# Expert attention: subtraction and row sums on VectorE, one exponential per eight heads, another order of pieces

## The chip, the core and the metric

The kernel runs on one NeuronCore of a Trainium2 chip. The metric is the device time of one execution in microseconds (us). Engines that matter here: TensorE (matmuls and transposes; PE in the rows, with PEld for its weight loads), VectorE (DVE), ScalarE (ACT), GpSimd (POOL) and SyncE (SP), which issues most transfers. Each engine works through its own queue in order, and engines wait for each other through semaphores.

## The reference, cut to what matters

Two decoder layers over 32 sequences of 112 tokens and 256 features. The last piece is a mixture of experts whose expert is a whole encoder layer; each sequence uses 2 of 4 experts, so there are 64 items (sequence, expert) to compute.

```python
def _encoder_layer(x, iw, ib, ow, ob, l1w, l1b, l2w, l2b, n1w, n1b, n2w, n2b):
    qkv = x @ iw.T + ib                        # 16 heads of 16
    scores = jnp.einsum('bhqd,bhkd->bhqk', q, k) / scale      # scale = 4
    attn = jax.nn.softmax(scores, axis=-1)
    o = jnp.einsum('bhqk,bhkd->bhqd', attn, v)...
    o = o @ ow.T + ob
    x = _layernorm(x + o, n1w, n1b)
    ff = jax.nn.relu(x @ l1w.T + l1b) @ l2w.T + l2b
    return _layernorm(x + ff, n2w, n2b)
gate_logits = x.mean(axis=1) @ gate_w.T + gate_b
_, top_idx = jax.lax.top_k(gate_logits, K)                    # K = 2
return jnp.einsum('be,ebsd->bsd', gate_weights * mask, expert_outs)
```

## The kernel before

The kernel has three stages, one after the other: the first layer, the first part of the second layer, and the experts. All is fp32. Only the third stage is touched.

In the third stage four lanes (`LANES`, 0 to 3) work through 16 items each (`share`). A lane has its own tiles, two PSUM banks (`bps0` to `bps3` in the profile) and its own copy of an expert's weights (`wexp`, `rexp`), which SyncE loads anew only where the next item of the lane has another expert. For one item of a lane:

- TensorE transposes the input (L1604), computes q and k feature-major (L1610) and v (L1626).
- VectorE adds the output bias to the input (L1819) and builds `QM`, q spread over masked heads (L1822, two instructions).
- For each of two groups of eight heads (`c`): TensorE computes the scores, 112x112 a head, into the lane's two banks (L1638). VectorE takes the maximum of each row (L1830, `mx`) and multiplies it by -0.25 (L1831, `low`). ScalarE computes exp(0.25 s + low), one instruction a head, with the row sum through its accumulator (L1716, `sums`); the profile shows an ACTIVATION_READ_ACCUMULATOR behind each. VectorE takes the reciprocal of the sums (L1834) and multiplies it in (L1835). TensorE transposes the probabilities (L1650), ScalarE copies them back (L1722).
- TensorE multiplies by v (L1658) and by the output weights (L1665). VectorE adds to the residual (L1840) and computes the layer norm: statistics (L1801, L1802), variance (L1803), normalisation (L1807, it waits for the inverse root that GpSimd computes, L1872), scale and shift (L1810, L1811), and the second bias (L1847).
- TensorE transposes (L1604) and runs the two layers of the feed-forward part (L1610 with ScalarE's relu L1739, and L1681). VectorE adds (L1850), does the second layer norm in the same way, multiplies by the gate (L1858), and GpSimd adds the item to the output by a transfer (L1885).

A half softmax below is what one lane does for one group of eight heads.

What an engine does for one item is written once, as a generator (`batch`) that yields between pieces. `run_slots` interleaves the four lanes' pieces on each engine: a piece of lane s is put at the turn (0 to 999) that the table `TURNS` gives for it, shifted by the lane's `lead3`. That makes the loop body; it runs 15 times. `FIRST` and `LAST` give the turns of what stands before the loop and behind it. So these tables alone set the order of the instructions on each queue. The rows named sp3, pe3, act3, dve3 and pool3 are the third stage's.

Semaphores that the change touches: `top_ready` (VectorE tells that the maxima are there), `exp_ready` (ScalarE tells that the exponentials are), `soft_ready`, and `s_psum` (the scores are in PSUM). The next scores may overwrite the banks, and the transposes may, once the exponentials have read them: TensorE waits for `exp_ready`.

Each VectorE instruction that needs the result of the one before it waits on a semaphore for it (`chained`).

Of the kernel before, what the change touches and what calls it, by code (L numbers as in the profile page):

```python
# [9 lines left out]
ALU = mybir.AluOpType  # L10
ACT = mybir.ActivationFunctionType
# [5 lines left out]
H = 16  # L17
# [23 lines left out]
def offsets(parts):  # L41
    at, out = 0, {}
    for name, w in parts:
# [122 lines left out]
            (),  # L166
            (),
            (820,)),
    "pe3": ((),
            (686, 763, 882, 982,),  # L170
            (526, 607, 687, 870, 944,),
            (236, 298, 399, 602, 745, 933, 973, 973,)),
    "act3": ((),
             (734, 885, 923,),
             (519, 587, 655, 887, 937,),
             (351, 427, 427, 598, 842, 930, 936, 964,)),
    "dve3": ((),
             (743, 886, 968,),
             (514, 666, 760, 816, 932,),
             (285, 497, 613, 613, 751, 914, 953,)),  # L180
    "pool3": ((),
              (),
              (960,),
              (878, 935, 961,)),
# [139 lines left out]
def build(nc, x, ctx, mask, wa, ca, ra, up, we, re_, gb, kc, kb, rtc, out, xmid, lg, mrow, sel, nb=B):  # L324
    with ExitStack() as es:
# [1110 lines left out]
        with ExitStack() as phase:  # L1436
# [40 lines left out]
            mx, low, sums, rec = lanes("mx", [T, H]), lanes("low", [T, H]), lanes("sums", [T, H]), lanes("rec", [T, H])  # L1477
# [107 lines left out]
            def _(pe):  # L1585
# [12 lines left out]
                def batch(s, at):  # L1598
# [30 lines left out]
                    for c in range(C2):  # L1629
                        yield  # L1630
                        if c == 0:
                            t.wait(masked_ready[s], 2)
                            t.wait(vx_read[s])
                        else:
                            t.wait(exp_ready[s])
# [5 lines left out]
                    for c in range(C2):  # L1641
                        yield
                        t.wait(soft_ready[s])
                        if c == 0:
                            t.wait(exp_ready[s])
                        else:
                            t.wait(pt_ready[s])
# [38 lines left out]
            def _(act):  # L1686
# [5 lines left out]
                def batch(s, at):  # L1692
# [17 lines left out]
                    for c in range(C2):  # L1710
                        yield
                        t.wait(top_ready[s])
                        for i in range(2):
                            for v in range(4):
                                h = 8 * c + 4 * i + v
                                m = A(PT[s][0:T, h, :], bank[s][i][0:T, v * T:(v + 1) * T], ACT.Exp, scale=0.25, bias=low[s][:, h:h + 1],  # L1716
                                      accum_out=sums[s][:, h:h + 1])
                        m.then_inc(exp_ready[s], 1)
# [25 lines left out]
            def _(dve):  # L1744
# [46 lines left out]
                def batch(s, at):  # L1791
# [34 lines left out]
                    for c in range(C2):  # L1826
# [4 lines left out]
                        v.tensor_scalar(low[s][:, eight], mx[s][:, eight], -0.25, None, ALU.mult).then_inc(top_ready[s], 1)  # L1831
                        yield
                        t.wait(exp_ready[s])
                        chained(v.reciprocal(rec[s][:, eight], sums[s][:, eight]))  # L1834
# [146 lines left out]
```

## Time and profile before

| | us |
|---|---|
| median of 3 runs | 3574.93 |
| lowest, highest | 3574.05, 3575.97 |
| profiled execution, its time | 3580.41 |
| profiled execution, its span | 3578.8 |
| busy in the span: matmuls | 3349.6 (94%) |
| VectorE | 2125.6 (59%) |
| ScalarE | 1943.2 (54%) |
| GpSimd | 375.7 (10%) |

The span runs from the first to the last instruction. The busy shares are averages over three stages with different loads. The third stage starts at about 2490 us and lasts to the end. A wait is put down to the instruction that released it. Matmuls are pipelined, and in the third stage each fp32 matmul of the code shows as two records.

### The profile page before, as it was taken

How to read it: one execution, taken by the hardware profiler on the slowest of the kernel's cores; microseconds unless marked ns; L12 is line 12 of the kernel's file. 1: busy time of each engine (PE TensorE's matmuls, PEld its weight loads, DVE VectorE, ACT ScalarE, POOL GpSimd, SP SyncE). 2: the span in 40 equal slices, each digit the busy share in tenths (PEclk: the TensorE clock that was granted, in tenths of full speed). 3: DMA queues.
4: the chain of work that ended last, by engine and by line, in shares of the span. 5: the costliest groups of instructions: out<-in, count | busy, mean ns of one | idle time of the engine just before them, and what ended most of it. 6: DMA issues, size and time to landing. Idle time of an engine off the chain costs nothing. (4 is left out here: it accounts for less than half of the span.)

```text
span 3578.8 us, 81208 instructions
## 1 busy us (share of the span) xinstructions
PE 3349.6 (94%) x30471; PEld 2507.5 (70%) x30471; DVE 2125.6 (59%) x6898; ACT 1943.2 (54%) x6528; POOL 375.7 (10%) x455
## 2 busy tenths in 40 slices
PE   6999999999799999999999999994999998999998
PEld 4777777777566666666666665663888887888887
DVE  4666666666444545454554545462777776777776
ACT  3655556555244444545454444542777775766775
POOL 1111111111000000000000000000011111111111
PEclk9999999999799999999999999997999999999999
DMA  2000000000200000000000000004100012120000
GB/s 82 13 13 17 13 13 13 14 15 8 98 7 22 18 18 22 18 22 18 22 18 20 19 15 25 15 2 144 56 14 15 13 35 60 29 58 14 14 13 13
DMA packets 63555, 94.47 MB, mean 26 GB/s; under 512 B 7763, under 2 KB 59603, under 8 KB 62147
## 3 DMA queue, kind: packets, MB, share of 16 engines
q1 hardware_dynamic: 55074, 83.41, 7.5%
q0 software_dynamic: 8224, 7.36, 1.8%
q8 instruction: 195, 3.19, 0.4%
q14 instruction: 62, 0.50, 0.0%
HBM read 72.07 MB, written 18.37 MB: 25 GB/s over the span
## 5 line engine op out<-in xcount | busy, mean ns | idle before, releaser
L1377 DVE CUSTOM_DVE_ANT_0 PON<-pps,PMR 112x375 f32<-112x375 f32 x512 | 259.7, 545 | 278.2 <-PE pps L1097 277.4
L1610 PE MATMUL bps<-BXT,Bwexp 128*128 128x112 f32 x3072 | 374.4, 279 | 15.1 <-DMA Bwexp<-in_we 7.5
L1610 PEld LDWEIGHTS bps<-BXT,Bwexp 128*128 128x128 f32 x3072 | 360.7, 194 | 36.9 <-ACT BXT L1732 15.9
L1716 ACT ACTIVATE BPT<-bps,Blow 112x112 f32<-112x112 f32 x1024 | 349.1, 392 | 15.2 <-DVE Blow L1831 14.7
L1230 ACT ACTIVATE PPT<-pps,mcol 125x896 f32<-125x896 f32 x192 | 193.3, 1007 | 196.9 <-PE pps L1116 196.4
L1716 ACT ACTIVATION_READ_ACCUMULATOR BPT<-bps,Blow 112x1 f32 x1024 | 250.1, 246 | 0.0
L1681 PE MATMUL bps<-Bwexp,BPT 128*112 128x256 f32 x1024 | 235.3, 381 | 0.0
L1097 PE MATMUL pps<-PKT,PQM 64*112 64x375 f32 x1024 | 226.4, 522 | 2.5 <-DVE Pmx L1377 1.5
L800 POOL TENSOR_TENSOR rstd<-var,nhalf 112x1 f32<-112x1 f32 (+1 forms) x96 | 149.5, 1557 | 745.3 <-DVE var L718 504.1
L1410 POOL TENSOR_TENSOR Prstd<-Pvar,nhalf 112x1 f32<-112x1 f32 x128 | 71.4, 560 | 1395.6 <-DVE Pvar L1297 1395.6
L643 ACT ACTIVATE PT<-PT,low 112x112 f32<-112x112 f32 x512 | 191.0, 384 | 36.3 <-DVE low L775 36.3
L1681 PEld LDWEIGHTS bps<-Bwexp,BPT 128*112 128x112 f32 x1024 | 176.2, 176 | 40.2
L1116 PE MATMUL pps<-PQM,PKT 64*125 64x448 f32 x768 | 187.4, 566 | 0.0
L1305 DVE TENSOR_TENSOR PX<-PX,pps 112x256 f32<-112x256 f32 x96 | 40.2, 419 | 229.0 <-PE pps L972 138.1
L1739 ACT ACTIVATE BPT<-bps,Bwexp 128x112 f32<-128x112 f32 x512 | 137.7, 386 | 35.0 <-PE bps L1610 35.0
L1872 POOL TENSOR_TENSOR Brstd<-Bvar,nhalf 112x1 f32<-112x1 f32 x128 | 74.2, 586 | 761.3 <-DVE Bvar L1803 761.3
L1722 ACT ACTIVATE BPT<-bps 112x896 f32<-112x896 f32 x128 | 120.5, 941 | 56.6 <-PE bps L1650 56.1
L1830 DVE TENSOR_REDUCE Bmx<-bps 112x8 f32<-112x896 f32 x128 | 139.0, 1086 | 19.2 <-PE bps L1638 18.0
L1835 DVE TENSOR_TENSOR BPT<-BPT,Brec 112x896 f32<-112x896 f32 x128 | 139.7, 1092 | 4.4
L474 PEld LDWEIGHTS ps<-CT,wa_sb 128*128 128x128 f32 x1024 | 131.7, 205 | 11.5 <-issue 1.6
L474 PEld LDWEIGHTS ps<-XT,wa_sb 128*128 128x128 f32 x1024 | 123.8, 198 | 21.4 <-issue 18.8
L1638 PE MATMUL bps<-BKT,BQM 64*112 64x112 f32 x2048 | 134.1, 270 | 4.0 <-ACT BPT L1716 2.4
(288 smaller groups left out, 7336.4 us busy)
## 6 DMA issues: line engine op xcount, KB each, us to landing
Bwexp<-in_we SPq DMA_DIRECT2D x7, 2304.0 KB, 15.7
PCX<-in_ctx SPq DMA_DIRECT2D x32, 375.0 KB
BXIN<-xmid SPq DMA_DIRECT2D x64, 112.0 KB
out<-BY POOLq DMA_DIRECT2D x64, 112.0 KB, 2.9
Bwexp<-in_we SPq DMA_DIRECT2D x7, 777.0 KB, 4.9
wa_sb<-in_wa SPq DMA_DIRECT2D x1, 4736.0 KB, 14.5
Brexp<-in_re SPq DMA_DIRECT2D x7, 672.0 KB
XIN<-in_x SPq DMA_DIRECT2D x32, 112.0 KB
```

What stands on the lines that cost most here:

```text
L474: m = mm(bk[:, j * T:(j + 1) * T], wt[:, c, m2 * 128:(m2 + 1) * 128], rhs[:, c, :], start=(c == 0), stop=(c == C2 - 1))
L643: m = A(PT[s][:, h, :], PT[s][:, h, :], ACT.Exp, bias=low[s][:, h:h + 1], accum_out=sums[s][:, h:h + 1])
L800: g.tensor_tensor(rstd[s][:, 0:n], var[s][:, 0:n], nhalf[0:T, 0:n], ALU.pow).then_inc(rstd_ready[s], 1)
L1097: m = mm(bank[s][i][0:T, 0:LC], QM[s][side[i], r // 4, r % 4, :], KT[s][side[i], r // 4, :], start=True, stop=True)
L1116: m = mm(bank[s][i][0:KP, 0:QW], KT[s][side[i], c, k * KP:(k + 1) * KP], QM[s][side[i], c, :, :], start=False, stop=True, skip_group_check ...
L1230: A(PT[s][0:KP, k, :, :].rearrange("p (i v) q -> p i (v q)", i=2), PS[s][0:KP, :, 0:QW], ACT.Exp, bias=mcol[:, k, bass.ds(at.n[s] + s * qu ...
L1377: m = v.tensor_tensor_reduce(out=ON[s][0:T, i * LC:(i + 1) * LC], in0=bank[s][i][0:T, 0:LC], in1=MR[s][:, :], scale=1.0, scalar=-3.0e38, o ...
L1610: m = mm(o[:, j * T:(j + 1) * T], wt[:, c, n0 + j * 128:n0 + (j + 1) * 128], rhs[:, c, :], start=(c == 0), stop=(c == 1))
L1681: m = mm(b0[0:T, 0:D], HT[s][:, mt, :], W(s, "l2", FT)[:, mt, :], start=(mt == 0), stop=(mt == FT - 1))
L1716: m = A(PT[s][0:T, h, :], bank[s][i][0:T, v * T:(v + 1) * T], ACT.Exp, scale=0.25, bias=low[s][:, h:h + 1], accum_out=sums[s][:, h:h + 1])
L1830: chained(v.tensor_reduce(mx[s][:, eight], PS[s][0:T, :, 0:QW].rearrange("p i (v k) -> p i v k", v=4), AX_X, ALU.max))
L1835: v.tensor_tensor(PT[s][0:T, eight, :], PT[s][0:T, eight, :], rec[s][:, eight].unsqueeze(2).to_broadcast((T, 8, T)), ALU.mult).then_inc(so ...
```

## The change

VectorE subtracts the row's maximum from the scores itself, out of PSUM into `PT` in SBUF, and then tells ScalarE; `low` is gone. ScalarE computes exp(0.25 x) over all eight heads of a group in one instruction, in place in `PT`, without an accumulator. VectorE then sums each row of the eight heads (a new instruction ahead of the reciprocal). TensorE waits for `top_ready` where it waited for `exp_ready`, since the banks have been read by then. The turns of the third stage are new for all five engines; stages one and two are as before. The loop, its 15 passes, the lanes, their leads and the matmuls are as before.

```diff
-    "dve3": ((42, 100, 249, 249, 371, 621, 631, 655, 833, 915,),
...
+    "dve3": ((0, 60, 148, 230, 289, 604, 605, 702, 859, 935,),
...
@@ the third stage's tiles
-            mx, low, sums, rec = lanes("mx", [T, H]), lanes("low", [T, H]), lanes("sums", [T, H]), lanes("rec", [T, H])
+            mx, sums, rec = lanes("mx", [T, H]), lanes("sums", [T, H]), lanes("rec", [T, H])
@@ TensorE, scores
                             t.wait(vx_read[s])
                         else:
-                            t.wait(exp_ready[s])
+                            t.wait(top_ready[s])
@@ TensorE, transposes
                         t.wait(soft_ready[s])
                         if c == 0:
-                            t.wait(exp_ready[s])
+                            t.wait(top_ready[s])
@@ ScalarE
                         t.wait(top_ready[s])
-                        for i in range(2):
-                            for v in range(4):
-                                h = 8 * c + 4 * i + v
-                                m = A(PT[s][0:T, h, :], bank[s][i][0:T, v * T:(v + 1) * T], ACT.Exp, scale=0.25, bias=low[s][:, h:h + 1],
-                                      accum_out=sums[s][:, h:h + 1])
+                        eight = slice(8 * c, 8 * c + 8)
+                        m = A(PT[s][0:T, eight, :], PT[s][0:T, eight, :], ACT.Exp, scale=0.25)
                         m.then_inc(exp_ready[s], 1)
@@ VectorE
                         chained(v.tensor_reduce(mx[s][:, eight], PS[s][0:T, :, 0:QW].rearrange("p i (v k) -> p i v k", v=4), AX_X, ALU.max))
-                        v.tensor_scalar(low[s][:, eight], mx[s][:, eight], -0.25, None, ALU.mult).then_inc(top_ready[s], 1)
+                        v.tensor_tensor(PT[s][0:T, eight, :].rearrange("p (i v) q -> p i v q", i=2), PS[s][0:T, :, 0:QW].rearrange("p i (v k) -> p i v k", v=4),
+                                        mx[s][:, eight].rearrange("p (i v) -> p i v", i=2).unsqueeze(3).to_broadcast((T, 2, 4, T)),
+                                        ALU.subtract).then_inc(top_ready[s], 1)
                         yield
                         t.wait(exp_ready[s])
+                        chained(v.tensor_reduce(sums[s][:, eight], PT[s][0:T, eight, :], AX_X, ALU.add))
                         chained(v.reciprocal(rec[s][:, eight], sums[s][:, eight]))
```

The order on VectorE in the middle of the loop body, where lane 1's second layer norm and lane 0's first one meet. The number behind a tile is its lane; Bst61 are the statistics of lane 1, Bst60 those of lane 0. Before:

```order
L1850 TENSOR_TENSOR BX1<-BPT1,bps1 112x256
L1801 BN_STATS Bst61<-BX1 112x6
L1802 BN_AGGR Bmv1<-Bst61 112x2
L1803 TENSOR_SCALAR Bvar1<-Bmv1 112x1
L1807 TENSOR_SCALAR BPT1<-BX1,Bmv1,Brstd1 112x256
L1810 TENSOR_TENSOR BPT1<-BPT1,Brexp1 112x256
```

The same place on VectorE after the change (L1798, L1799, L1800 and L1804 are what L1801, L1802, L1803 and L1807 were):

```order
L1850 TENSOR_TENSOR BX1<-BPT1,bps1 112x256
L1798 BN_STATS Bst61<-BX1 112x6
L1799 BN_AGGR Bmv1<-Bst61 112x2
L1800 TENSOR_SCALAR Bvar1<-Bmv1 112x1
L1833 TENSOR_REDUCE Bsums3<-BPT3 112x8
L1834 RECIPROCAL Brec3<-Bsums3 112x8
L1835 TENSOR_TENSOR BPT3<-BPT3,Brec3 112x896
L1840 TENSOR_TENSOR BX0<-BX0,bps0 112x256
L1798 BN_STATS Bst60<-BX0 112x6
L1799 BN_AGGR Bmv0<-Bst60 112x2
L1800 TENSOR_SCALAR Bvar0<-Bmv0 112x1
L1804 TENSOR_SCALAR BPT0<-BX0,Bmv0,Brstd0 112x256
```

Lane 1's normalisation stood right behind its variance; now lane 3's row sum, reciprocal and multiplication and lane 0's first statistics come between. Lane 0's own normalisation stands right behind its variance.

The order on VectorE late in the loop body, at lane 2's and lane 1's scores. Before:

```order
L1819 TENSOR_TENSOR BX1<-BXIN1,Brexp1 112x256
L1822 SCALAR_TENSOR_TENSOR BQM1<-bps1,Bwexp1,hm4 128x448 x2
L1834 RECIPROCAL Brec2<-Bsums2 112x8
L1835 TENSOR_TENSOR BPT2<-BPT2,Brec2 112x896
L1830 TENSOR_REDUCE Bmx2<-bps2 112x8
L1831 TENSOR_SCALAR Blow2<-Bmx2 112x8
L1850 TENSOR_TENSOR BX0<-BPT0,bps0 112x256
```

The same place on VectorE after the change:

```order
L1816 TENSOR_TENSOR BX1<-BXIN1,Brexp1 112x256
L1819 SCALAR_TENSOR_TENSOR BQM1<-bps1,Bwexp1,hm4 128x448 x2
L1833 TENSOR_REDUCE Bsums2<-BPT2 112x8
L1834 RECIPROCAL Brec2<-Bsums2 112x8
L1835 TENSOR_TENSOR BPT2<-BPT2,Brec2 112x896
L1827 TENSOR_REDUCE Bmx1<-bps1 112x8
L1828 TENSOR_TENSOR BPT1<-bps1,Bmx1 112x896
L1827 TENSOR_REDUCE Bmx2<-bps2 112x8
L1828 TENSOR_TENSOR BPT2<-bps2,Bmx2 112x896
L1850 TENSOR_TENSOR BX0<-BPT0,bps0 112x256
```

Each half softmax has one instruction more here (the row sum, L1833), and the subtraction L1828 in the place of L1831; lane 1's maximum stands ahead of lane 2's second one, and both are ahead of lane 0's addition.

## Rows read from the trace of the kernel before

**Rows 1.** Windows: one round of the third stage; busy us (instructions) of each engine.

```profile
core 0: us, PE busy (x) PEld busy (x) DVE busy (x) ACT busy (x) POOL busy (x), PEclk, DMA share, GB/s
2559.01:2624.38 65.37, 64.36 (x626) 55.73 (x626) 48.02 (x109) 46.51 (x201) 7.78 (x12) 1.00 0.09 15
```

**Rows 2.** Chain of waits, third stage, longest pieces: start us, us, what.

```profile
2559.01 6.86 issue
...
2573.78 2.81 ACT BPT L1716 x16
...
2624.34 6.89 issue
...
2951.03 9.27 DMA Brexp<-in_re
...
3493.03 6.88 issue
```

**Rows 3.** Waits of VectorE, 2559 to 2951 (six rounds): total us, times, longest.

```profile
DVE BX L1850 <- PE bps L1681: 42.8, 24, 3.0
DVE BPT L1807 <- POOL Brstd L1872: 24.0, 36, 1.1
DVE BX L1819 <- SPq L1547: 9.0, 6, 1.5
DVE BX L1840 <- PE bps L1665: 4.0, 6, 0.7
...
DVE Bmx L1830 <- PE bps L1638: 1.6, 6, 0.3
```

**Rows 4.** Timeline of VectorE, 2803.5 to 2810: start us, us, what, [idle before].

```profile
2804.66 0.20 DVE L1834 RECIPROCAL Brec<-Bsums 112x8 f32<-112x8 f32 x1
2804.89 1.09 DVE L1835 TENSOR_TENSOR BPT<-BPT,Brec 112x896 f32<-112x896 f32 x1
2805.90 1.08 DVE L1830 TENSOR_REDUCE Bmx<-bps 112x8 f32<-112x896 f32 x1
2807.01 0.17 DVE L1831 TENSOR_SCALAR Blow<-Bmx 112x8 f32<-112x8 f32 x1
2807.09 0.42 DVE L1840 TENSOR_TENSOR BX<-BX,bps 112x256 f32<-112x256 f32 x1
...
2808.23 0.15 DVE L1803 TENSOR_SCALAR Bvar<-Bmv 112x1 f32<-112x1 f32 x1
2809.07 0.41 DVE L1807 TENSOR_SCALAR BPT<-BX,Bmv,Brstd 112x256 f32<-112x256 f32 x1 [0.69 <-POOL Brstd L1872]
```

**Rows 5.** Groups of VectorE, 2559 to 2951: busy us, mean ns | idle before.

```profile
L1835 DVE TENSOR_TENSOR BPT<-BPT,Brec 112x896 f32<-112x896 f32 x48 | 52.4, 1092 | 1.6
L1830 DVE TENSOR_REDUCE Bmx<-bps 112x8 f32<-112x896 f32 x48 | 52.1, 1085 | 2.0 <-PE bps L1638 1.6
...
L1831 DVE TENSOR_SCALAR Blow<-Bmx 112x8 f32<-112x8 f32 x48 | 8.2, 171 | 1.6
```

**Rows 6.** Groups of VectorE by form, 0 to 2600 us, stages one and two.

```profile
L1305 DVE TENSOR_TENSOR PX<-PX,pps 112x256 f32<-112x256 f32 x96 | 40.2, 419 | 229.0 <-PE pps L972 138.1 <-PE pps L1025 71.8 <-issue 18.2
...
L713 DVE TENSOR_TENSOR KX<-ps,ca_sb 128x448 f32<-128x448 f32 x64 | 39.6, 618 | 20.9 <-PE ps L474 20.9
...
L717 DVE TENSOR_REDUCE var<-SQ 112x20 f32<-112x320 f32 x32 | 15.4, 482 | 9.4 <-ACT SQ L609 9.4
```

**Rows 7.** Groups of ScalarE, 2559 to 2951.

```profile
L1716 ACT ACTIVATE BPT<-bps,Blow 112x112 f32<-112x112 f32 x384 | 131.0, 395 | 5.3 <-DVE Blow L1831 5.1
L1716 ACT ACTIVATION_READ_ACCUMULATOR BPT<-bps,Blow 112x1 f32 x384 | 94.7, 249 | 0.0
```

**Rows 8.** Groups of ScalarE by form, 0 to 2600 us.

```profile
L627 ACT ACTIVATE PT<-PT 112x896 f32<-112x896 f32 x64 | 57.1, 941 | 0.0
```

**Rows 9.** Waits of the matmuls, 2559 to 2951: total us, times, longest.

```profile
PE bps L1650 <- ACT BPT L1716: 2.9, 6, 0.5
```

**Rows 10.** Windows of 10 us while the third stage fills.

```profile
2500.00:2510.00 10.00, 6.03 (x62) 4.93 (x60) 5.94 (x12) 7.20 (x40) 0.00 (x0) 1.00 1.00 424
```

More of the change, by code:

```diff
@@ L165 @@
     "sp3": ((),
-            (),
-            (),
-            (820,)),
[3 rows of a table added]
     "pe3": ((),
-            (686, 763, 882, 982,),
-            (526, 607, 687, 870, 944,),
-            (236, 298, 399, 602, 745, 933, 973, 973,)),
[3 rows of a table added]
     "act3": ((),
-             (734, 885, 923,),
-             (519, 587, 655, 887, 937,),
-             (351, 427, 427, 598, 842, 930, 936, 964,)),
[3 rows of a table added]
     "dve3": ((),
-             (743, 886, 968,),
-             (514, 666, 760, 816, 932,),
-             (285, 497, 613, 613, 751, 914, 953,)),
[3 rows of a table added]
     "pool3": ((),
-              (),
-              (960,),
-              (878, 935, 961,)),
[3 rows of a table added]
 }
```

91 rows, old and new, of tables (FIRST, LAST, TURNS) are left out of this document.

## The prediction, before the changed kernel had run

> **What bounds the kernel now.** I read the table of windows first. The change touches only the expert stage, the last 1,090 us of the span. Its steady part is a loop that repeats every 65.4 us, four items (one for each lane) a time; I call that a round [rows 1]. The chain of waits shows the same spot of the loop at 2559.01 and at 2624.34, and the last such spot at 3493.03 [rows 2]. The loop runs 15 times, the sixteenth item of each lane lies in what runs before and behind it.
>
> In one round the matmuls are busy 64.36 of 65.37 us at the full clock, VectorE 48.02, ScalarE 46.51 [rows 1]. So TensorE sets the round, and VectorE has room. How much room, the busy share does not say: between two instructions of VectorE lie small gaps that no other work fills. I take instead the round less what VectorE really waits for. In six rounds it waits 42.8 us for the second layer's matmuls (L1850), 24.0 for the inverse root of GpSimd (L1807), 9.0 for the clearing of the semaphores by the DMA queue (L1819), 4.0 and 1.6 for other matmuls [rows 3]: 81.4 us, or 13.6 a round. VectorE's own work thus takes 65.37 - 13.57 = **51.8 us a round**.
>
> **The change, part by part.** A round has eight half softmaxes (four items, two groups of eight heads); all of VectorE's and ScalarE's counts below are for one of them.
>
> Removed from VectorE: the scaling into `low` (L1831). It starts at 2807.01 and the next, independent instruction at 2807.09 [rows 4], so it takes up 0.08 us of the queue, though 171 ns by itself [rows 5].
>
> Added to VectorE: the subtraction, 112x896 from PSUM into SBUF. The trace has none of this form. The nearest is the multiplication L1835, 112x896 in SBUF, 1,092 ns [rows 5], with 1.01 us from its start to that of the next, independent one (2804.89 to 2805.90) [rows 4]. That PSUM as a source costs no more is seen from smaller ones: 112x256 with PSUM takes 419 ns and 128x448 618 ns [rows 6], 1.04 ns a column, which gives 1.08 us at 896. I take 1.01; nothing that depends on it stands behind it on its queue at once. Bounds: 1.00 (1.08 less the overlap of 0.08 that the multiplication shows) and 1.12 (if its successor had to wait for its end, as L1831 waits for L1830).
>
> Added to VectorE: the sum over each row, 112x896 to 112x8 out of SBUF. The maximum L1830 is the same reduction out of PSUM, 1,085 ns [rows 5]; a reduction out of SBUF of 320 columns takes 482 ns [rows 6], the line through both has 1.05 ns a column, so SBUF is not faster. The reciprocal needs its result, so it counts from start to dependent start, as 2805.90 to 2807.01 does: 1.11 to 1.12 us [rows 4]. Bounds: 1.00 and 1.12. The Trainium skill, "VectorE: DVE Perf Modes", section "The DRAIN you can't avoid", says that a semaphore after each VectorE instruction costs nothing extra, since the next one is held until the pipe is empty anyway. The rows speak against it: 1.11 us to a dependent instruction, 1.01 to an independent one of equal length [rows 4]. By the page the sum would count 1.01, a round would be 0.9 us shorter and the kernel 13 us faster than my forecast.
>
> Sum for a half softmax: 1.01 + 1.12 - 0.08 = 2.05 us (1.92 to 2.16). Eight of them: **16.4 us a round** (15.4 to 17.3). VectorE's work becomes 51.8 + 16.4 = **68.2 us** (67.2 to 69.1), more than the 65.4 of TensorE. VectorE takes over as the bound.
>
> ScalarE: eight exponentials with eight reads of the accumulator, 131.0 + 94.7 us of overlapping records in six rounds [rows 7], 2.81 us from first to last [rows 2], give way to one exponential over 112x896. That form exists in the first stage (L627), 941 ns [rows 8]. ScalarE falls from 46.5 by 8 x 1.87 to about 31.5 us a round. It bounds nothing before or after, so this saves nothing by itself. Nor does the path through one half softmax get shorter: before 1.12 + 0.17 + 2.81 + 0.23 + 1.09 = 5.4 us, after 1.12 + 1.09 + 0.94 + 1.12 + 0.23 + 1.09 = 5.6 us.
>
> TensorE: no matmul comes or goes. The scores' banks come free with the subtraction, not with the exponential, some 2 us earlier. It waits for the exponential 2.9 us in six rounds [rows 9], half a microsecond a round; that goes, and is worth nothing once VectorE is the bound.
>
> The new order of pieces decides how much of VectorE's old waiting comes on top of the 68.2. Inverse root: before, six normalisations in a round stand right behind their variance and wait 0.69 us or so each (2808.23, next 2809.07) [rows 3, 4]. Now, in the order of after, a subtraction, a multiplication or a row sum stands between in all places but one (lane 0 after its first layer norm): 0.7 us a round. Clearing of the semaphores, 1.5 us each time [rows 3]: each lane now has 2 us of other work between its last write and its next start, so it is covered. Second layer: from the normalisation of lane 3 to the addition that needs its matmuls I count 10.6 us of VectorE's work; TensorE's part is about 9 us, so covered with little to spare. Row sum: in two places four short instructions (1.2 us) stand between the subtraction and its row sum, with the subtraction 2.2 us, against 1.09 + 0.94 us and two hand-overs: just covered. TensorE now has 4 us of slack a round to be ahead of VectorE. Before, the bounding engine lost 1.0 us a round [rows 1]. I take 0.7 + 0.6 = 1.3 us of loss (0.7 to 3.5): a round of **69.5 us**, 4.1 more than before. 15 rounds: +62 us.
>
> Outside the steady rounds: filling and draining hold the other eight half softmaxes, 0.2 us longer each on a path and 2 us heavier for VectorE; +2 (-2 to +8). When an expert's weights change, the start of a lane waits for its row of constants, 9.27 us in the worst place [rows 2]; there the write of an item was followed at once by the next start on the same lane, now 2 to 6 us of work lie between: -5 (-8 to 0) in all. Sum: 62 + 2 - 5 = **+59 us**. The profiled execution took 3580.41 us, so it would take 3639; the median of the runs lies 5.5 us under it, 3574.93 + 59 = **3634 us** (+1.65%).
>
> **Rivals.**
> A. VectorE is the bound, but the two orders interlock worse: with both queues at 90% and over, a late matmul holds a row sum, which holds the next. For it: the thin margins above, and that VectorE's queue now has hardly a gap to catch up. Against: TensorE's slack. A loss of 5 us a round instead of 1.3 gives 73.2, so +117 - 3: 3689 us. It begins at a loss of 3.5.
> B. TensorE stays the bound, the added work is hidden. For it: 48 of 65 us busy looks like room. It needs an added 1.70 us or less a half softmax instead of 2.05, under both lower bounds. Then the round is 65.4 and only the cover at the changes of experts is won: 3570 us.
> C. Faster, by one mechanism: the exponential leaves TensorE's path (-0.5 us a round, [rows 9]), and the bound stays at TensorE as in B: 3574.93 - 7.5 - 5 = 3562 us. It decides from the same point as B.
> D. The round isn't bound by an engine but by a ring of dependent steps through VectorE; then every added microsecond counts in full: 65.4 + 16.4 = 81.8 a round, 3821 us. Against it: matmuls wait only 1.0 us a round [rows 1]. The Trainium skill, "Perfetto Trace Analysis", section "Identifying the Most-Contended Engine", calls the matmuls' busy share a bad measure, and wants the share of weight loads; that is 55.73 of 65.37, 85% [rows 1], and by it TensorE had 15% of room, which would make room for D.
> E. TensorE's clock falls because it waits more. Against: in 2500 to 2510 us it was busy 6.03 of 10 us, and the granted clock was 1.00 [rows 10]. I fold it into A.
>
> **Numbers.** Forecast 0.71 (3600 to 3668), A 0.15, B 0.05, C 0.05, D 0.04. The forecast's own range: low with 67.2 + 0.7 a round and 8 us of cover, 3574.93 + 15 x 2.5 - 10 = 3602; high with 69.1 + 3.0, which is 15 x 6.7 + 5: 3680. The range is 3602 to 3680 and takes in the start of A. A measurement of this kernel tells 0.2% (7 us) from no change. Faster 0.06, within 0.2% 0.04, slower 0.90.
>
> **What would show it.** In the profile of after: a steady round of 69 to 70 us, VectorE busy 64 to 65 us of it (48.0 + 16.4 with fewer gaps), its waits for matmuls (L1850) near zero, matmuls busy 64.4 with idle time now put down to VectorE, ScalarE busy near 32. The subtraction 1.08 to 1.10 us, the row sum 1.09, the exponential 0.94. Wrong if a round stays at 65.4 (B, C: then the added instructions must be under 0.9 us), if VectorE still waits over 3 us a round (A), or if the row of constants is waited for as long as before.

## The result, and the profile after

The changed kernel takes 3608.57 us (median of four runs, 3603.62 to 3611.82), the kernel before 3575.45 (four runs, 3574.05 to 3578.70): a ratio of 1.0096, 95% interval 1.0084 to 1.0109. It is 33 us slower. The forecast was 59 slower, with a range of 3602 to 3680. The profiled execution of after has a span of 3610.2 us, that of before 3578.8, so the profiles differ by 31.4.

The windows of two steady rounds of after (columns as in [rows 1]):

```profile
2562.09:2629.37 67.28, 64.89 (x627) 55.38 (x626) 62.86 (x117) 32.73 (x80) 7.87 (x13) 1.00 0.09 14
2831.20:2898.48 67.28, 64.94 (x626) 55.32 (x625) 62.86 (x117) 32.73 (x80) 7.86 (x13) 1.00 0.08 14
```

A round takes 67.28 us instead of 65.37. VectorE went from 48.02 to 62.86 us busy, ScalarE from 46.51 to 32.73, the matmuls stayed near 64.9. Alone, this row doesn't say which engine sets the round; the chain of waits does, by the share of the whole span that each engine has in it (page of after):

```profile
DVE 20%; issue 8%; PE 1%; DMA 1%; POOL 1%; SPq 0%; DVEq 0%; ACT 0%; POOLq 0%
```

The same line of before reads "PE 18%; DVE 5%". The pieces of this chain in the third stage (start us, us, what), to be laid beside [rows 2]. The long "issue" piece comes back once a round at the same spot of the loop; I call it the mark:

```profile
2562.09 7.21 issue
...
2629.34 7.24 issue
...
2965.78 13.59 issue
...
3054.65 7.84 DMA Brexp<-in_re
...
3225.02 4.37 DMA Bwexp<-in_we
...
3522.80 7.24 issue
```

From the first mark to the last, 14 rounds later, are 960.71 us; before it was 3493.03 - 2559.01 = 934.02. That is 26.69 more, and 14 x (67.28 - 65.37) = 26.7. The stage's steady part starts 3.1 us later than before, and what lies behind the last mark is 87.4 us long instead of 85.8. So 3.1 + 26.7 + 1.6 = 31.4 us, the whole difference of the spans.

All waits of VectorE that the profile names from 2562.09 to 2965.78, six rounds (total us, times, longest), which answer to [rows 3]:

```profile
DVE BPT L1804 <- POOL Brstd L1872: 4.0, 6, 0.7
DVE BX L1816 <- DVE BPT L1847: 3.7, 12, 0.3
DVE BY L1858 <- DVE BPT L1808: 3.5, 18, 0.3
```

The second and third are VectorE waiting for its own instruction before. Of the 81.4 us of waits in six rounds before, 4.0 are left: one inverse root a round, 0.67 us. VectorE's queue is full: 67.28 - 0.67 = 66.6 us a round are its own work. Its costliest groups in the same six rounds (answers to [rows 5]), and the exponential (answers to [rows 7]):

```profile
L1835 DVE TENSOR_TENSOR BPT<-BPT,Brec 112x896 f32<-112x896 f32 x49 | 53.5, 1092 | 1.7
L1828 DVE TENSOR_TENSOR BPT<-bps,Bmx 112x896 f32<-112x896 f32 x48 | 52.4, 1092 | 1.7
L1827 DVE TENSOR_REDUCE Bmx<-bps 112x8 f32<-112x896 f32 x48 | 52.0, 1083 | 0.2
L1833 DVE TENSOR_REDUCE Bsums<-BPT 112x8 f32<-112x896 f32 x48 | 51.7, 1078 | 0.2
```

```profile
L1714 ACT ACTIVATE BPT<-BPT 112x896 f32<-112x896 f32 x48 | 45.8, 954 | 33.8 <-DVE BPT L1828 33.1
```

And a piece of VectorE's timeline, to be laid beside [rows 4]:

```profile
2829.47 1.08 DVE L1833 TENSOR_REDUCE Bsums<-BPT 112x8 f32<-112x896 f32 x1
2830.58 0.20 DVE L1834 RECIPROCAL Brec<-Bsums 112x8 f32<-112x8 f32 x1
2830.82 1.09 DVE L1835 TENSOR_TENSOR BPT<-BPT,Brec 112x896 f32<-112x896 f32 x1
2831.83 1.08 DVE L1827 TENSOR_REDUCE Bmx<-bps 112x8 f32<-112x896 f32 x1
2832.94 1.09 DVE L1828 TENSOR_TENSOR BPT<-bps,Bmx 112x896 f32<-112x896 f32 x1
2833.95 0.41 DVE L1807 TENSOR_TENSOR BPT<-BPT,Brexp 112x256 f32<-112x256 f32 x1
```

The row sum takes 1.11 us to the start of the reciprocal that needs it (2829.47 to 2830.58), the subtraction 1.01 to the start of an independent instruction (2832.94 to 2833.95). Both are the prices of the forecast, to 0.01 us.

### The profile page after: what moved, and what is told of

It is laid out like the page before. It is cut to its first block and busy times, and to the rows that moved or that the text cites. A ratio compares the mean times of both kernels' runs of the same rounds, so it can differ in the third digit from the quotient of the medians.

```text
span 3610.2 us, 79400 instructions
## 1 busy us (share of the span) xinstructions
PE 3363.0 (93%) x30471; PEld 2507.7 (69%) x30471; DVE 2364.7 (66%) x7026; ACT 1721.2 (48%) x4608; POOL 376.5 (10%) x455
## 5 line engine op out<-in xcount | busy, mean ns | idle before, releaser
L1610 PE MATMUL bps<-BXT,Bwexp 128*128 128x112 f32 x3072 | 384.2, 282 | 26.8 <-SPq L1531 14.6
L1610 PEld LDWEIGHTS bps<-BXT,Bwexp 128*128 128x128 f32 x3072 | 365.9, 196 | 51.4 <-issue 26.5
L1681 PE MATMUL bps<-Bwexp,BPT 128*112 128x256 f32 x1024 | 235.5, 379 | 0.0
L1681 PEld LDWEIGHTS bps<-Bwexp,BPT 128*112 128x112 f32 x1024 | 174.0, 176 | 35.4
L1714 ACT ACTIVATE BPT<-BPT 112x896 f32<-112x896 f32 x128 | 122.0, 954 | 93.3 <-DVE BPT L1828 91.8
L1719 ACT ACTIVATE BPT<-bps 112x896 f32<-112x896 f32 x128 | 117.0, 914 | 98.6 <-PE bps L1650 98.6
L1835 DVE TENSOR_TENSOR BPT<-BPT,Brec 112x896 f32<-112x896 f32 x128 | 139.8, 1092 | 4.4
L1828 DVE TENSOR_TENSOR BPT<-bps,Bmx 112x896 f32<-112x896 f32 x128 | 139.7, 1092 | 4.4
L1833 DVE TENSOR_REDUCE Bsums<-BPT 112x8 f32<-112x896 f32 x128 | 138.0, 1078 | 5.3 <-ACT BPT L1714 4.8
```

The source lines that it names most:

```text
L1610: m = mm(o[:, j * T:(j + 1) * T], wt[:, c, n0 + j * 128:n0 + (j + 1) * 128], rhs[:, c, :], start=(c == 0), stop=(c == 1))
L1681: m = mm(b0[0:T, 0:D], HT[s][:, mt, :], W(s, "l2", FT)[:, mt, :], start=(mt == 0), stop=(mt == FT - 1))
L1828: v.tensor_tensor(PT[s][0:T, eight, :].rearrange("p (i v) q -> p i v q", i=2), PS[s][0:T, :, 0:QW].rearrange("p i (v k) -> p i v k", v=4), ...
L1833: chained(v.tensor_reduce(sums[s][:, eight], PT[s][0:T, eight, :], AX_X, ALU.add))
L1835: v.tensor_tensor(PT[s][0:T, eight, :], PT[s][0:T, eight, :], rec[s][:, eight].unsqueeze(2).to_broadcast((T, 8, T)), ALU.mult).then_inc(so ...
```

## The experiments

My theory, called V in the expectations: VectorE's queue is the bound, and each microsecond on it counts in full. Against it stand an interlock of the in-order queues (the prediction's rival A), TensorE as a floor, and theory O, by which the added work is cheap and the new order of pieces causes the loss. All times are medians; the ratios are to the kernel before on the same chip.

### Is VectorE's queue the bound? Take the row sum out, or put it in twice

The first kernel (e3) leaves the row sums out and takes the reciprocals of the maxima in their place:

```
-   chained(v.tensor_reduce(sums[s][:, eight], PT[s][0:T, eight, :], AX_X, ALU.add))
-   chained(v.reciprocal(rec[s][:, eight], sums[s][:, eight]))
+   chained(v.reciprocal(rec[s][:, eight], mx[s][:, eight]))
```

> The changed kernel without the row sums; the reciprocal is taken of the maxima, so the probabilities are not normalised. Takes 8 x 1.11 = 8.9 us a round out of VectorE's queue. Theory V: VectorE's work 57.7 us, TensorE bounds at its busy 64.4 us and a little waiting, a round of 64.6 to 65.4: 15 x 2.3 us less than the changed kernel, 3565 to 3582 us, and only a quarter of the 8.9 us shows. Theory R (a ring of dependent steps runs through VectorE, each microsecond counts in full): 3608 - 133 = 3475 us. Theory O: 3600 us or more.

The second kernel (e4) repeats after's row sum as it stands:

```
    chained(v.tensor_reduce(sums[s][:, eight], PT[s][0:T, eight, :], AX_X, ALU.add))
+   chained(v.tensor_reduce(sums[s][:, eight], PT[s][0:T, eight, :], AX_X, ALU.add))
```

> The changed kernel with each row sum done twice. Adds 8 x 1.11 = 8.9 us a round to VectorE's queue. Theory V: it shows in full, a round of 76.2 us, 3608 + 15 x 8.9 + 3 = 3745 us (3730 to 3760), and matmuls idle for 11 us a round. If VectorE were only nearly full (slack left in its waits): under 3720 us.

Measured: without it 3572.1 us (ratio 0.9990, 0.9979 to 1.0001), with two 3748.57 (1.0488, 1.0467 to 1.0510). Windows of 260 us of the first, then of the second:

```profile
2560.00:2820.00 260.00, 256.26 (x2498) 222.51 (x2497) 218.79 (x432) 130.39 (x321) 33.43 (x48) 1.00 0.09 14
```

```profile
2560.00:2820.00 260.00, 227.21 (x2154) 193.02 (x2153) 243.31 (x421) 111.99 (x275) 26.42 (x40) 0.99 0.08 13
```

The chain of waits of the first, then of the second, over neighbouring rounds:

```profile
2626.51 6.87 issue
...
2691.55 6.86 issue
```

```profile
2564.41 8.33 issue
...
2640.54 8.36 issue
```

Two sums: a round of 76.13 us, 8.85 more than after's 67.28; that is 8 x 1.11, the timeline's price of one sum. Every microsecond shows. No sum: 65.04, only 2.24 less, although 8.9 of work went. There the matmuls are busy 256.26 of 260 us, and VectorE waits again (VectorE's waits in the same 260 us of that kernel):

```profile
DVE BX L1849 <- PE bps L1681: 10.5, 16, 1.1
DVE Brec L1833 <- ACT BPT L1714: 10.5, 8, 1.7
```

So TensorE's floor is 65.0 us a round in this order too, and after stands 2.2 above it, on VectorE's side. Without the row sum its VectorE would need 66.6 - 8.9 = 57.7. Theory O falls here in one half: the new order by itself doesn't hold the round above 65.0.

### A small weight: leave one addition out

After without its addition of the second bias (e10, L1847):

```
-   chained(v.tensor_tensor(Z[s][:, :], Z[s][:, :], rr(s, "l2b"), ALU.add))
```

> The changed kernel without the addition of the feed-forward part's output bias to the residual (L1847, 112x256, 0.46 us from start to start, four a round), so the result lacks that bias. It takes 1.84 us a round from VectorE, near the point where TensorE takes over. Theory V: VectorE's work 64.8 + 0.7 of wait = 65.5 us against TensorE's 65.0, so nearly all of it shows: 15 x 1.8 = 27 us less than the changed kernel, 3581 us (3575 to 3587). If TensorE held the round back by itself already: 3595 us or more.

Measured: 3588.79 us (1.0034, 1.0020 to 1.0049). That is 20 us under after; a full count of 4 x 0.46 us would be 26 to 28. A round has 65.98 us (the chain's mark stands at 2621.52, 2687.51, 2753.49), and the window shows both engines nearly full:

```profile
2560.00:2820.00 260.00, 254.70 (x2475) 218.58 (x2474) 241.81 (x443) 128.27 (x313) 31.50 (x48) 1.00 0.08 13
```

VectorE's need falls to 66.6 - 1.8 + 0.7 = 65.5, and 65.98 come out, half a microsecond above VectorE's 65.5 and 1.0 above TensorE's 65.0. Half of that half is a wait which after doesn't have: VectorE waits for exponentials (L1714) 1.0 us in these 260, 0.25 a round. The rest is small pieces that the profile doesn't name. In this kernel the corner between the two bounds is round, not sharp. The time, 3588.79, lies just above the 3575 to 3587 expected.

### The order apart from the code

The new code with the tables of before (e1; one row of them is shown), and the old code with the tables of after (e2), the same edit the other way round:

```
-    "pe3": ((0, 25, 33, 260, 369, 450, 497, 733, 821, 898, 932, 977, 977, 977,),
+    "pe3": ((6, 24, 111, 176, 372, 481, 569, 688, 758, 907, 927, 928, 963, 963,),
```

> The changed code in the order of the kernel before (its turns for the third stage). Theory V (VectorE's own work, 66.6 us a round, bounds the changed kernel, and the new order is what keeps its waits at 0.7 us): the old order has six normalisations right behind their variance (24.0 us in six rounds before) and a start right behind a write (9.0 us in six rounds), so 66.6 + 4.0 + 1.5 = 72 us a round, 15 x 4.8 us more than the changed kernel: 3680 us (3650 to 3710). Theory O (the added work is cheap, and the loss of 33 us comes from the new order): this is faster than the changed kernel, 3575 to 3600 us.

> The code of the kernel before in the new order. Theory V: VectorE's work is 50 us a round and TensorE bounds again; the order was not made for eight exponentials of 2.8 us, so a round of 65.4 to 67: 3575 to 3600 us, with VectorE waiting for ScalarE's exponentials. Theory O: the order carries the loss, so about 3608 us, or above.

Measured: new code in the old order 3696.54 us (1.0339, 1.0319 to 1.0358), old code in the new order 3818.15 (1.0667, 1.0641 to 1.0693). The first is 88 us slower than after with the same instructions. Its window and VectorE's two largest waits in it:

```profile
2640.00:2900.00 260.00, 236.65 (x2222) 205.55 (x2221) 225.73 (x411) 116.58 (x284) 26.69 (x41) 0.97 0.08 12
```

```profile
DVE BPT L1804 <- POOL Brstd L1872: 14.6, 22, 1.1
DVE BX L1816 <- SPq L1547: 4.5, 3, 1.5
```

A round took 72.6 us (L1804 at 2717.76 and 2790.35). Over 260 us, 3.58 rounds, the inverse root costs 4.1 us a round and the clearing 1.3, the two waits that the old order leaves on VectorE's queue [rows 3]. With the 66.6 of work that makes 72.0 of the 72.6. So for the changed code the new order does what I read out of it: it puts other work over the inverse roots and the clearing. It saves 5.3 us a round in all; of these, 4.1 + 1.3 less the 0.7 that after still pays, 4.7, are these two waits. That is the other half of theory O refuted: the old order makes the new code slower, not faster.

The old code in the new order was the clearest miss. VectorE has no more to do there than in before, 50.3 us a round. The window, and two waits in it:

```profile
2640.00:2900.00 260.00, 224.12 (x1979) 191.55 (x1979) 152.69 (x346) 147.08 (x625) 25.04 (x38) 0.91 0.07 12
```

```profile
DVE Brec L1834 <- ACT BPT L1716: 52.5, 14, 9.9
...
PE bps L1638 <- ACT BPT L1716: 18.3, 10, 3.9
```

No engine is full, and a round took 81.9 us (2702.63 to 2784.48). The chain of waits runs from engine to engine (start us, us, what):

```profile
2712.07 0.97 PE bps L1638 x16
...
2714.26 3.84 PE bps L1610 x32
2718.12 1.09 ACT BPT L1739 x4
2719.21 2.70 ACT BPT L1716 x16
2722.05 1.15 PE bps L1650 x8
```

On ScalarE's queue the exponentials (L1716) stand behind the relu (L1739), which waits until 2718.12 for TensorE's L1610; TensorE's next transposes (L1650) wait for the exponentials, because these read the bank that the transposes write; and the matmuls of the next relu stand behind the transposes on TensorE's queue. In after one exponential of 0.95 us stands in that place and no longer holds the bank. Here eight take 2.70, and the delay is handed from queue to queue. It is rival A's mechanism, an interlock, but in a kernel that is neither before nor after. The chain shows that the queues hand the delay on; which of the two, the length of the exponentials or the held bank, costs how much is the question of e5 below.

### One half of the code change at a time

Each half in either order. Only the subtraction on VectorE, eight exponentials with accumulators, no row sum; the shape of the edit to after's code, in after's order (e5), for the first group of eight heads alone (e6), and in before's order (e8):

```
-   m = A(PT[s][0:T, eight, :], PT[s][0:T, eight, :], ACT.Exp, scale=0.25)
+   for h in range(8 * c, 8 * c + 8):
+       m = A(PT[s][0:T, h, :], PT[s][0:T, h, :], ACT.Exp, scale=0.25, accum_out=sums[s][:, h:h + 1])
...
-   chained(v.tensor_reduce(sums[s][:, eight], PT[s][0:T, eight, :], AX_X, ALU.add))
```

> The changed kernel in its order, but with eight exponentials per half softmax that sum through ScalarE's accumulator, and no row sum on VectorE (the subtraction stays there). VectorE's work is 57.7 us as without row sums; each exponential step lasts 2.8 instead of 0.95 us. Theory L (the kernel before in the new order was slow, 3818 us, since the new order has no room for a long exponential ahead of the reciprocal): slow here too, 3650 to 3800 us. Theory K (it was slow since TensorE had to wait for the exponential before it could use the banks again): here the subtraction frees the banks, so 3572 to 3590 us.

> The changed kernel in its order; only the first group of eight heads of each item sums through ScalarE's accumulator (eight exponentials), the second keeps one exponential and the row sum on VectorE. VectorE's work 66.6 - 4 x 1.11 = 62.2 us a round. Theory V: under TensorE's 64.4, so TensorE bounds: 65.0 us as without any row sums, 3572 us (3566 to 3585). By theory L part of the longer exponentials is waited for: 3590 to 3700 us.

> The kernel before in its own order, with the subtraction on VectorE (TensorE waits for it in place of the exponential) and eight exponentials with accumulators out of SBUF. The other part alone. Theory V: VectorE's work 50.3 + 8 x 0.93 = 57.7 us and up to 5.5 of waits, 63.2, under TensorE's 65.4: 3568 to 3585 us. In proportion: 3590 us or more.

Only the row sum on VectorE, with eight exponentials from PSUM without accumulators; e7 in after's order (its expectation says "its own", but the kernel has after's tables, so it stands beside e2), e9 in before's:

```
-   m = A(PT[s][0:T, h, :], bank..., ACT.Exp, scale=0.25, bias=low[s][:, h:h + 1],
-         accum_out=sums[s][:, h:h + 1])
+   m = A(PT[s][0:T, h, :], bank..., ACT.Exp, scale=0.25, bias=low[s][:, h:h + 1])
...
+   chained(v.tensor_reduce(sums[s][:, eight], PT[s][0:T, eight, :], AX_X, ALU.add))
```

> The kernel before in its own order, with the row sums on VectorE and without accumulators on ScalarE; low and the eight exponentials out of PSUM stay. One part of the change alone. Theory V: VectorE's work 50.3 + 8.9 = 59.2 us and up to 5.5 us of waits that the old order has behind variances and writes: 64.7, just at TensorE's 65.4: 3575 to 3600 us. If each part cost by itself in proportion: 3592 us or more.

> The kernel before, in its own order, with the row sums on VectorE and without accumulators; low and the eight exponentials out of PSUM stay. (The run e7 had the same code in the new order.) Theory V: VectorE's work 50.3 + 8.9 = 59.2 us and up to 5.5 us of waits behind variances and writes, 64.7, just under TensorE's 65.4; the step from the maximum to the probabilities lasts 0.3 us longer: 3575 to 3605 us. Theory P (every added instruction costs in proportion, wherever the bound is): 8.9 us a round of the 16.3 would cost 18 us in the new order, 65 us here: 3640 us.

Measured: e5 3627.65 (1.0156), e6 3617.47 (1.0128), e8 3600.67 (1.0081), e7 3721.91 (1.0411), e9 3628.13 (1.0145), each within 0.0023 either way. By VectorE's load all had room: e5 and e8 come to 57.7 us of work a round, e6 to 62.2, e7 and e9 to 59.2, all under the 65.0 of TensorE. The load sum put e5, e6, e8 and e9 between 3566 and 3605, and each came out above its own range; e6 and e8 came out in the range of the rival set against it (L for e6, in proportion for e8), e5 and e9 between theirs.

e5 was to tell why e2 is slow: by theory L the order has no room for long exponentials (3650 to 3800 us), by theory K the exponentials hold the banks that TensorE needs (3572 to 3590), and in e5 the subtraction frees these. Neither range holds. VectorE's and TensorE's largest waits in e5:

```profile
DVE Brec L1833 <- ACT BPT L1714: 25.6, 14, 3.0
```

```profile
PE bps L1658 <- ACT BPT L1719: 11.0, 8, 1.5
```

e3 has the same order, the same 57.7 us of work on VectorE and the same release of the banks, and one exponential in the place of eight: there the two waits are 10.5 and 1.2 us, and the round is 65.0. The longer exponentials alone, accumulators included, thus cost 3.5 us a round. What is held up in e2 and not in e5 is TensorE: in e2 its scores and transposes wait 18.3 + 10.4 us in 260 for the exponentials, 9.0 a round; in e5 the profile names no such wait. How much of e2's round this makes by itself isn't shown.

The window of e8 and VectorE's largest waits:

```profile
2560.00:2820.00 260.00, 250.58 (x2417) 216.94 (x2417) 213.41 (x421) 169.52 (x790) 30.04 (x47) 1.00 0.08 13
```

```profile
DVE BPT L1804 <- POOL Brstd L1871: 15.9, 24, 1.1
DVE BX L1849 <- PE bps L1681: 12.3, 8, 1.8
```

The waits are the ones of before [rows 3]; what is new is that TensorE, full before, now has 3.6% of idle time. A round is 66.99 us (2605.93 to 2672.92). VectorE's own 57.7 plus 4.1 of inverse roots, 1.2 of clearing and 3.2 for matmuls is 66.2: its added work no longer all fits into the places where it used to wait. I read this so, that those waits stand elsewhere in its queue than the work that was added; no run here tests that reading. e9 has the same waits and rounds of 67.9 us twice (2589.99, 2657.91, 2725.81) and 70.9 next.

e7 against e2 points the same way as e5. Without accumulators eight take 1.97 us instead of 2.70 (chain of e7: "2700.26 1.97 ACT BPT L1716 x8"); the round falls from 81.9 to 75.0 although VectorE has 8.9 us more to do. In e5 eight of them out of SBUF take 2.22 to 2.34, and a round takes 68.5. After, with one of 0.95, has 67.3.

### Less work than before, and still slower

After without the maxima and the subtraction, which leaves out the shift by the maxima: the exponential reads PSUM itself, and TensorE's next scores and transposes wait for it (`exp_ready`) again.

```
-   t.wait(top_ready[s])
-   m = A(PT[s][0:T, eight, :], PT[s][0:T, eight, :], ACT.Exp, scale=0.25)
+   t.wait(s_psum[s])
+   m = A(PT[s][0:T, eight, :].rearrange("p (i v) q -> p i (v q)", i=2), PS[s][0:T, :, 0:QW], ACT.Exp, scale=0.25)
...
-   chained(v.tensor_reduce(mx[s][:, eight], PS[s][0:T, :, 0:QW]..., AX_X, ALU.max))
-   v.tensor_tensor(PT[s]..., PS[s]..., mx[s]..., ALU.subtract).then_inc(top_ready[s], 1)
```

> The changed kernel without maxima and subtraction: one exponential per eight heads straight from PSUM, row sums on VectorE (the same function as long as no exponential overflows). VectorE's work 66.6 - 8 x 2.12 = 49.6 us a round, ScalarE's 32. Theory V: TensorE bounds as in the run without row sums; a round of 64.4 to 65.0 and no more than that to gain, however much is taken off VectorE: 3560 to 3575 us. It gives the floor of this stage on TensorE. If VectorE's queue still mattered: under 3550 us.

Measured: 3624.19 us (1.0131, 1.0114 to 1.0148), 16 slower than after, with about 17 us of VectorE's work a round taken away. The expectation, 3560 to 3575, missed: it went by the load alone. Window, and the two largest waits of VectorE:

```profile
2560.00:2820.00 260.00, 249.23 (x2382) 215.07 (x2373) 179.19 (x383) 122.15 (x304) 30.10 (x46) 0.98 0.08 13
```

```profile
DVE BX L1845 <- PE bps L1681: 30.3, 7, 5.4
DVE Bsums L1828 <- ACT BPT L1714: 19.6, 8, 4.1
```

VectorE waits in the open for the second layer and for exponentials, up to 5.4 us at a time, where after has no such wait; and TensorE itself idles 4% and is granted 0.98 of its clock. Rounds are 68.6, 68.5, 67.0 and 68.6 us (L1681 at 2624.61, 2693.17, 2761.67, 2828.65, 2897.23). The waits show that VectorE's load doesn't set the round; why the steps come late, whether by the order alone or by the banks held longer, isn't shown.

All kernels side by side, VectorE's own work by load sum (after's 66.6 and the timeline's prices) and the round:

```
kernel                       order    VectorE's work   round
row sum twice      (e4)      after        75.5         76.1
after                        after        66.6         67.3
new code           (e1)      before       66.6         72.6
no second bias     (e10)     after        64.8         66.0
first group accum. (e6)      after        62.2         67.9
row sum alone      (e7)      after        59.2   72 to 75
row sum alone      (e9)      before       59.2   68 to 71
subtraction alone  (e5)      after        57.7         68.5
subtraction alone  (e8)      before       57.7         67.0
no row sum         (e3)      after        57.7         65.0
before                       before       50.3         65.4
old code           (e2)      after        50.3         81.9
no maxima          (e11)     after        49.6         68.5
```

In after's order with after's exponential and waits (e4, after, e10, e3) the round is the larger of VectorE's work + 0.7 and 65.0, to half a microsecond. Two of the four, after and e3, give the numbers of this sum; e4 and e10 test it. Wherever the length or the releaser of the exponential differs from what an order was made for, the same sum is a floor and nothing more.

## Why the prediction was right, and by how much it missed

**The bound changes.** Right. The prediction had VectorE take over from TensorE; its named waits fell from 81.4 to 4.0 us in six rounds, and a doubled row sum shows in full (8.85 us a round of 8.9).

**The prices.** Right. Subtraction 1.01 and row sum 1.11 to 1.12, less 0.08: 2.04 a half softmax, 16.3 a round against the 16.4 forecast. I had quoted the Trainium skill, "VectorE: DVE Perf Modes", section "The DRAIN you can't avoid", by which the row sum would count 1.01. The result lies nearer to the 13 us less that I worked out from it, but not for that reason: after's timeline has 1.11 to the dependent reciprocal, and the doubled sum adds 8.85 us a round, 1.11 each, where 1.01 would have added 8.1. There the second sum reads nothing that the first one wrote and waits only for its semaphore, so the 0.1 us go with the wait and not with the data. What the page says of the semaphore, measured there on copies, doesn't hold for these rows.

**VectorE's own work, a term that was mis-sized.** I took the round less its waits, 51.8 us, and added 16.3: 68.1. It was 66.6, 1.5 less. Busy time shows the same: it grew by 14.84, not by 16.3. Most of it is the tail of an instruction with a wait behind it. VectorE before:

```profile
2823.04 1.08 DVE L1830 TENSOR_REDUCE Bmx<-bps 112x8 f32<-112x896 f32 x1
2824.16 0.17 DVE L1831 TENSOR_SCALAR Blow<-Bmx 112x8 f32<-112x8 f32 x1
2825.98 0.42 DVE L1850 TENSOR_TENSOR BX<-BPT,bps 112x256 f32<-112x256 f32 x1 [1.65 <-PE bps L1681]
```

L1831 counts 0.17 us in front of a wait, but 0.08 where the next instruction is ready [rows 4]; the last 0.08 to 0.09 us of an instruction run beside its successor. Before, 13 instructions a round stood in front of a wait (24 + 36 + 6 + 6 + 6 in six rounds [rows 3]), now one: 12 x 0.08 = 1.0 us. The other 0.5 I can't assign from the rows. Worked back from after, the work before was 66.6 - 16.3 = 50.3 in a queue without waits; the tails alone would give 50.8 and a round of 67.8, where 67.3 came. I had put a bound on each new instruction, but none on the 51.8.

**Losses of the new order.** I had 0.7 us for one exposed inverse root and 0.6 more on the model of TensorE's losses before. The first was there at the place named (lane 0 after its first layer norm):

```profile
2842.61 0.86 DVE L1804 TENSOR_SCALAR BPT<-BX,Bmv,Brstd 112x256 f32<-112x256 f32 x2 [0.67 <-POOL Brstd L1872]
```

The second was zero. The clearing, the second layer and the row sums are covered as worked out; none is in the list of waits. (What I called the clearing by the DMA queue is a wait for SyncE: L1547 is its word that the lane's row of constants is in place, given behind the clearing. The sum doesn't hang on the name.) Together, 1.5 + 0.6 + 0.1 make the 2.2 us by which 69.5 was too high; over 14 rounds that is 31 us.

**Outside the rounds.** I gave +2 for filling and draining; it was 3.1 + 1.6 = 4.7, within the bounds. The cover at the changes of expert, -5, did not come: 960.71 - 14 x 67.28 is 18.8 us of stalls, and before 934.02 - 14 x 65.37 = 18.8 as well. The worst stall shrank from 9.27 us for the row of constants to 7.84, but the rounds with a change of expert are as long in all: by the marks, three of them take 6.4, 5.8 and 6.6 us more than 67.28 (from 2965.78, 3039.43 and 3179.78), where before two had 16.0 together and a third 3.1 more than 65.37. The step that failed is that I priced the cover at one stall and took the sum of all to follow it. My sign of being wrong, "if the row of constants is waited for as long as before", came true in effect for this term. I also counted 15 rounds where the marks hold 14; the fifteenth is in the drain. In the profile's own terms the forecast of 59 was 27.6 above the 31.4: 31 from the 2.2 us a round, 4.1 from the fifteenth round, less 5 for the cover and 2.7 for the ends, 27.4 in all. The missing cover and the ends took back 7.7 of the 35 us that the rounds and the miscount were too high; that much of the closeness is luck.

**Rivals.** A, the interlock, was not in this kernel (0.67 us of waits against its 3.5), but it rules the neighbours, e2 and e7 above all. B and C fall with the prices: 2.04 us a half softmax against the 1.70 they need. D falls in its own form, since 16.3 added us moved the round by 1.9. The Trainium skill's rule that I set beside it ("Perfetto Trace Analysis", section "Identifying the Most-Contended Engine": not by the matmuls' busy share but, beside the share of peak arithmetic, by that of the weight loads) gave TensorE 15% of room by the weight loads. The kernel without row sums shows 222.51 of 260 us of weight loads, 86%, and yet TensorE holds the round at 65.0, with matmuls busy 98.6%; here the matmuls' share came nearer. It isn't sure by itself either: in after, where VectorE sets the round, the matmuls still show 64.89 of 67.28 us, 96.5%. E, the clock: 1.00 in after's rounds, as said, but 0.97 and 0.91 in e1 and e2.

**Forecasts of the profile.** ScalarE 32.73 a round (forecast 31.5 to 32), subtraction 1,092 ns (1.08 to 1.10), row sum 1,078 (1,090), exponential 954 (940), VectorE busy 62.86 (64 to 65, off by the tails), matmuls 64.9 (64.4). The idle time of the matmuls, which I had put down to VectorE, goes to it only in part: 4.2 us in six rounds to L1819, but 6.1 to SyncE's word that the lane's weights are in place (L1531).

**What stays open.** No kernel with the full computation beat the one before. Whether an order made for one of the halves (e5, e8, e9) would bring it under 3575 wasn't tried; the load sums say there is room, the runs only that neither of the two orders here finds it.

## What to carry to other kernels

To move work to an engine with spare time, take its work from the round less its waits, subtract about 0.08 us for each wait that will go, add the new instructions by start-to-start distances (behind a wait or not), and compare with the present bound; near the crossing the round comes out longer than either (0.5 us in e10). That sum holds only for an order of the queues made for the new lengths: with the same instructions, a foreign order cost 88 and 243 us here. A part of a change tried alone in an order made for the whole says little about the part.

## What was unexpected of the hardware

- The eight exponentials of 112 columns take 2.81 us (first to last) out of PSUM with accumulators [rows 2], 1.97 without (e7), 2.22 to 2.34 out of SBUF with accumulators (e5); one of 896 columns takes 0.95. So the accumulators cost about 0.1 us an instruction, the split into eight another 1 us.
- The granted clock of TensorE was 1.00 in after's rounds (2.4 GHz throughout), 0.97 in e1 and 0.91 in e2 as means over 260 us, so a part of that time at 1.2 GHz. It doesn't follow the matmuls' share: e5 has them busy 243.33 of 260 us at 1.00, e11 249.23 at 0.98. In e2 it fell behind stretches in which the matmuls stood still, and came back under full work (windows as in [rows 1]):

```profile
2766.00:2768.00 2.00, 0.00 (x0) 0.00 (x0) 1.75 (x7) 2.00 (x14) 0.65 (x1) 0.76 0.00 0
...
2770.00:2772.00 2.00, 2.00 (x12) 1.82 (x9) 1.90 (x4) 0.00 (x0) 0.00 (x0) 0.50 0.51 57
...
2774.00:2776.00 2.00, 2.00 (x21) 1.55 (x23) 0.64 (x2) 1.51 (x4) 0.00 (x0) 1.00 0.00 0
```

  In e2's window of 260 us a matmul takes 224.12 / 1979 = 113 ns, without the row sum 256.26 / 2498 = 103. Of e2's 16.5 us more a round, about 6.7 are this by my estimate (626 matmuls x 10.7 ns, all of it put down to the clock), the rest are waits.
- An exponential of 896 columns is no slower out of PSUM than out of SBUF: 923 ns in e11, 954 in after.
